# A two-layer transformer kernel: half of the first chunk's inverse loads issued from ScalarE's queue, and the next row's deviation taken between two steps of the last inversion

## The reference

```
h = layernorm(x) * (1 + ca) + sa
x = x + ga * attention_0(h)          # 16 heads of 8, causal softmax
h = layernorm(x) * (1 + cb) + sb
x = x + gb * experts_0(h)            # 8 experts, the top 2 of each token
h = layernorm(x) * (1 + ca) + sa     # second layer, own shifts and scales
x = x + ga * gated_delta_net(h)      # 12 heads, keys of 64, values of 128
h = layernorm(x) * (1 + cb) + sb
x = x + gb * ffn_1(h)                # 128 -> 512 -> 128, gelu
```

```
S = S * exp(gt); kv = kt . S; delta = (vt - kv) * bt
S = S + kt x delta; ot = qt . S
```

## Time and profile before

| | |
|---|---|
| median of three runs | 2789.67 us |
| the profiled execution | 2795.61 us |
| its span, first to last instruction | 2793.9 us |
| mean granted TensorE clock | 0.961 |
| TensorE busy (matmuls) | 2440.6 us, 87% |
| VectorE busy | 1793.1 us, 64% |
| ScalarE busy | 1453.6 us, 52% |
| GpSimd busy | 824.7 us, 30% |
| DMA engines, mean rate | 50 GB/s |

### The profile page before, as it was taken

The page is one execution under the profiler, slowest core; times in us unless marked ns, Lnnn a source line. Parts: engine busy times, 40 slices in busy tenths (PEclk is TensorE's granted clock), DMA queues, the critical chain, the costliest instruction groups (busy, mean ns, idle before and its releaser), DMA issues.

```text
span 2793.9 us, 65708 instructions
## 1 busy us (share of the span) xinstructions
PE 2440.6 (87%) x24090; PEld 1704.2 (61%) x24299; DVE 1793.1 (64%) x4697; ACT 1453.6 (52%) x3129; POOL 824.7 (30%) x581
## 2 busy tenths in 40 slices
PE   3898989899898988989889898898988989889997
PEld 2456755477554875547755577555774567655675
DVE  3467764777737766378664786557765678646776
ACT  0465534755448543385434754447544574446643
POOL 3045210552106511065100552015420253204521
PEclk8999999999999989999899998999999999999999
DMA  8201131010310103101130011300132011220113
GB/s 276 81 3 20 16 100 73 4 22 13 104 69 10 19 14 115 55 12 19 22 128 32 13 19 44 132 5 16 16 101 78 1 19 19 95 78 2 20 16 99
DMA packets 226986, 138.32 MB, mean 50 GB/s; under 512 B 173567, under 2 KB 209799, under 8 KB 219431
## 3 DMA queue, kind: packets, MB, share of 16 engines
q1 hardware_dynamic: 221670, 126.26, 16.1%
q10 hardware_dynamic: 4980, 7.60, 0.7%
HBM read 95.10 MB, written 38.71 MB: 48 GB/s over the span
## 4 chain that ended last, share of the span: by engine, by line
PE 50%; DVE 18%; ACT 15%; issue 9%; DMA 4%; SPq 3%; POOL 1%; DVEq 0%; ACTq 0%; POOLq 0%
PE bank L914 7%; PE bank L699 4%; PE bank L509 3%; PE bank L952 3%; PE bank L1013 3%; PE bank L690 3%; DVE small L1367 3%; PE bank L622 3%; ACT arena L1638 2%; ACT arena L1637 2%; PE bank L1033 2%; ACT vq L1645 2%; DVE blk_tx L1369 2%; DVE mx L1171 2%; PE bank L547 2%
## 5 line engine op out<-in xcount | busy, mean ns | idle before, releaser
L1912 POOL TENSOR_TENSOR arena<-upto,gk 128x1536 f32<-128x1536 f32 x32 | 88.1, 2752 | 679.2 <-DVE beta L1308 679.2
L1315 DVE SCALAR_TENSOR_TENSOR arena<-bank,conv,arena 128x510 f32<-128x510 f32 x320 | 237.1, 747 | 44.8 <-ACT arena L1638 27.2
L1171 DVE TENSOR_REDUCE mx<-bank 128x2 f32<-128x768 f32 (+3 forms) x187 | 202.1, 1123 | 56.6 <-PE bank L548 55.1
L509 PE MATMUL bank<-mask_k,ident_bf 128*128 128x512 bf16 x848 | 221.7, 389 | 17.4 <-issue 15.8
L1904 POOL TENSOR_TENSOR arena<-arena 128x511 f32<-128x511 f32 x160 | 201.6, 1270 | 56.8 <-DVE arena L1315 56.8
L1601 ACT ACTIVATE arena<-bank 128x384 f32<-128x384 f32 (+1 forms) x384 | 168.5, 547 | 49.1 <-PE bank L607 49.0
L760 PE MATMUL bank<-h_pad,arena 128*128 128x512 f32 x320 | 165.6, 615 | 28.5 <-DVE arena L1315 21.7
L547 PE MATMUL bank<-vq 128*128 128x128 bf16 (+3 forms) x528 | 122.0, 315 | 56.0 <-issue 35.7
L1367 DVE TENSOR_TENSOR small<-blk_tx,blk 96x1 f32<-96x1 f32 (+14 forms) x480 | 142.7, 297 | 16.5
L1622 ACT ACTIVATE arena<-bank,b1e 128x512 f32<-128x512 f32 x128 | 87.8, 686 | 116.8 <-PE bank L690 111.7
L1276 DVE SCALAR_TENSOR_TENSOR arena<-bank,comb,arena 128x128 f32<-128x128 f32 x256 | 72.1, 344 | 114.8 <-PE bank L699 113.7
(11 more groups left out here) (300 smaller groups left out, 5949.0 us busy)
## 6 DMA issues: line engine op xcount, KB each, us to landing
vq<-q_rows SPq DMA_DIRECT2D x18, 1024.0 KB, 8.5
vq<-k_rows SPq DMA_DIRECT2D x18, 1024.0 KB, 11.4
arena<-w_bounce SPq DMA_DIRECT2D x16, 1024.0 KB, 6.0
q_rows<-qkp SPq DMA_DIRECT2D x81, 128.0 KB, 2.4
k_rows<-qkp SPq DMA_DIRECT2D x81, 128.0 KB, 2.4
arena<-wv_rows SPq DMA_DIRECT2D x8, 768.0 KB, 10.2
ogt<-wv_rows SPq DMA_DIRECT2D x8, 768.0 KB, 11.8
t_bounce<-blk_tx SPq DMA_DIRECT2D x32, 192.0 KB, 2.1
```

The lines of the kernel that those rows point to most:

```text
L509: mm(PS[bank][:, :], ident_bf[:, :], mask_k[:, :, :].rearrange("p h w -> p (h w)"), start=True, stop=True)
L1171: V.reduce_max(dst, unit_scores(u), AX.X).then_inc(s_max, 1)
L1315: ins = V.scalar_tensor_tensor(a[:, k:T], ps[:, 0:T - k], conv[:, n, 3 - k:4 - k], a[:, k:T], ALU.mult, ALU.add)
```

## The change

There are two edits.

First, for chunk 0 alone, SP issues only the loads of the first four blocks. The other four are issued by ScalarE's queue, in a new function `load_inverses` that waits for `t_out` just as SP does. It is called right behind `direct(3)`. So that it can stand there, the copy that stood between `direct(3)` and the end of the loop moves behind it.

Second, ScalarE's `enter_stats` for the next row leaves its place behind `levels(3)` and is now called inside it, ahead of step 6.

```diff
@@ act_stages
-        act_stages += [("gate", 2), ("levels", 3), ("enter_stats", 1), ("rms", 2), ("enter_norm", 1), ("enter_h", 1), ("gate", 3),
+        act_stages += [("gate", 2), ("levels", 3), ("rms", 2), ("enter_norm", 1), ("enter_h", 1), ("gate", 3),
@@ ScalarE
+                def load_inverses():
+
+                    act.wait_ge(t_out, at(b, t_out, 16))
+                    for q in range(NBK // 2, NBK):
+                        r, d = slice(BS * q, BS * (q + 1)), slice(BS * q % DK, BS * q % DK + BS)
+                        act.dma_start(tx16[r, :, :, d].rearrange("p h s k -> p (h s) k"),
+                                      t_bounce[q].rearrange("h s i k -> i (h s) k")).then_inc(t_in, 16)
+
@@ convolve, ScalarE
-                        if n >= NQK + 2:
+                        if n >= NQK + 2 and n < NQK + 7:
                             copy_v(n - NQK - 2)
                         if n == NQK + 3:
                             first_tap(NCT - 1)
+                        elif n == NQK + 7:
+                            load_inverses()
                     if i == 2:
+                        copy_v(NTOK - 3)
                         copy_v(NTOK - 2)
                         copy_v(NTOK - 1)
@@ levels, ScalarE
                     for s in range(3, 8):
+                        if s == 6 and c + 1 == NT:
+                            enter_stats(b, 1)
@@ SP
-                    for q in range(NBK):
+                    for q in range(NBK if c else NBK // 2):
```

## The result

| | before | after |
|---|---|---|
| median, range, runs | 2788.68 us, 2783.77 to 2790.66, 4 | 2740.86 us, 2734.56 to 2749.12, 4 |
| the profiled execution, its span | 2795.61 us, 2793.9 us | 2734.56 us, 2732.8 us |
| mean granted TensorE clock | 0.961 | 0.976 |
| TensorE busy | 2440.6 us | 2433.6 us |

The ratio of after to before is 0.9834, 95% interval 0.9806 to 0.9862. The changed kernel is 47.8 us faster (38.5 to 54.1 by the interval). The forecast was 34.3 us; the time came out 4 us under the low end of the range.

The account below looks back on a forecast made before the run. TensorE was taken to bound the kernel, pausing for the first inversion's loads and the next row's normalised tokens. Gains of 17.1 + 17.2 = 34.3 us from the 2789.67 us median gave 2755 us, range 2745 to 2775.

Parts of the forecast that it names:

- both mechanisms: First inversion's loads: issues split over two queues, gain 17.1 us; next row's entry: earlier deviation, gain 17.2 us.
- the clock term: Behind both pauses: slow products may run faster once the pause is gone, 1.25 us a time; none counted.
- the bound of 27.2 us: Next row's entry: upper gain of the second edit if the pause makes the clock fall, 1.25 us more a time.
- the two terms: Clock terms at loads and entry; half of both, 5 + 5 us, gave the forecast's own low end, 2745 us.
- For the spread of the rows I leave 0.3 us a time: First inversion's loads: wait left after the first edit, cutting its gain from 19.5 to 17.1 us.
- the prediction's worst case of 3.8: First inversion's loads: a load lands at most 3.8 us after its issue began, leaving up to 0.75 us of wait.
- Rival A: First inversion's loads: the two queues take turns issuing, gain 3.6 us in place of 17.1, 2769 us; chance 0.20.
- Rival B: Next row's entry: the clock keeps half of the second gain, leaving 8.6 us, 2764 us; chance 0.13.
- Rival C: Behind either place: the gain comes back as another wait, at `blk` or the next chunk's mask, 2788 to 2790 us; chance 0.08.
- Rival D: First inversion's loads: long issues on ScalarE's queue hold its copies, kernel 7.8 us slower, 2797 us; chance 0.04.

## Why the prediction was right and where it was wrong

**The direction and both mechanisms were right.** Issuing was what was long at the loads, ScalarE's idle time hid its four issues, the deviation had its statistics before step 6, TensorE had nothing else to wait for, and no later wait took the gain back.

**The step that failed** is the clock term, at both places: "At most 8 x 1.25 = 10 us come back if the pause is gone. I count none of it." And for the second edit the bound of 27.2 us was written down and 17.2 taken. The prediction had read the clock at one place, behind the pause; ahead of it the clock was already at 0.51. The filled waits show that this term is real. At the loads it is 4.8 us, half of the 10, since in four of the eight rows the clock had not fallen. At the entry the pause itself is 17.2 us and the stages gave 31.1, so about 14 are clock, 12 of them behind the transposes; with the wait kept and filled 22 us came back behind the transposes, 16 net. The 14 are above the 10 us that the gate's products suggested: 8 us came back in the part with these products, 2 ahead of the transposes and 4 behind the next layer norm. The single timings of the second edit, 24 us, leave 7 for the clock. Sum of what was not counted: some 19 us by the stages. A row of full speed and a row of half speed for the same work stood beside each other in the evidence for the loads, and that was the ground to take half of the two terms at the least, which would have been 2745 us, the low end of the range.

**A second step was mis-sized the other way.** "For the spread of the rows I leave 0.3 us a time": it is 6.1 / 8 = 0.77 us. The issues began on time, but with two queues at work a load of ScalarE's lands a median of 2.6 us after its issue began, not 2.1, and its fourth, which ends the wait, 3.4 to 3.9 us after: near the prediction's worst case of 3.8 in every row, with a long issue or without. The pauses gave 13.4 us and not 17.1. The two errors partly cancel: 13.4 + 4.8 = 18.2 us at the first place, near the forecast's 17.1, for other reasons.

**Rival A,** two queues taking turns, is refuted: ScalarE's first three issues, 0.36 and 0.49 us long, lie in the same 1.4 us in which SP issued its own three. The trace does not show what the Trainium skill's "Perfetto Trace Analysis", section on the HWDGE DMA instruction, would lead to here, that a descriptor generator locked for one queue's instruction delays the other's. The rule of the Trainium skill's "DMA: Bandwidth & Descriptors", section "Issuing engines are not separate DMA queues", agrees with the trace: what was saved is issuing time, and a load did not land sooner (median 2.2 us for the first chunk's loads before, 2.1 for SP's and 2.6 for ScalarE's after). **Rival B,** half of the second gain lost to the clock, had the sign wrong in its sum: the work behind the transposes became 12 us shorter, not 8.6 us longer. What it feared did occur in part: the clock fell ahead of the pause in six of the 8 rows before, and a slow stretch is left at the entry in five of the 8 rows of the changed kernel. It is shorter: around the entry the clock was at half for 65 us over the rows before and for 24 after. **Rival C** did not occur: VectorE's second substitution starts 5.85 us behind the inversion's start (1226.27 - 1220.42), before 7.08 (1259.34 - 1252.26), so it came forward with the chain and more. **Rival D** did not occur with four loads and did with seven.

**Chance and place.** The inversion of the third chunk took 291.1 us in the profiled execution of before and 280.5 in that of after. Over kernels with that same place of the code it lies anywhere from 274.9 to 291.1 us, with either edit or none, so these 10.6 us lie within the scatter between executions and cannot be credited to the change. What they come from, a stall at that place of the program, is worth 15 us by the means of that stage.

**The best version** is the changed kernel with 8 unread products in the prologue, 2726.73 us, or with the rest of the pause filled, 2726.44; by their ratios of 0.977 and 0.978 they are one and the same. They are 14 to 16 us below the changed kernel's 2740.86 and 2742.84 as the times stand, and 14 to 24 by the ratios. Of that the stage of the third inversion gives 10 to 19 us, by the place of the code; no other stage got shorter.

**What stays open.** Which property of the place makes TensorE stall was not found; 8 and 16 instructions (a weight load and a product for each) work alike. The kernels before with 8 and 4 products gained 8 and 12 us in time where the stage gave 15, which is at or inside the ends of their intervals (2.5 to 15.3 and 8.1 to 21.5); nothing here tells whether a rest is missing. What makes the clock fall ahead of the entry's pause was not tried, nor where the long issue comes from, nor why ScalarE's fourth load lands late.

## What to carry to other kernels

Price a pause of TensorE as its length plus what the clock takes behind it: find the same products at full and at half speed in the trace, multiply the difference by how often the slow form occurs, and count that. Look also where the clock falls: at the entry it fell ahead of the pause in most rows, and part of the slow stretch stayed when the pause went. If a pause can't be shortened, filling it with unread products brings the second part alone (4.8 and 16 us here, beside 18 and 31 for removing it); size the fill by what it takes at half the clock, or it holds the work behind it, as it did here by 5 to 7 us. And before a gain of an added instruction is believed, put as many instructions where they do nothing: here a fill that seemed to bring 14 us brought none.

## What the runs showed of the hardware

SP's and ScalarE's queues issue DMAs at full pace at the same time (medians 467 and 490 ns); a long issue of 1.4 to 1.8 us then falls on the fourth of both at once in four of 8 rows, and ScalarE's fourth load lands 3.4 to 3.9 us after its issue began in all of them. In this kernel removing a pause of 2.2 us at the entry took off some 1.8 us more in slow products (14 us over 8 rows, from the stages of single executions). And 8 or 16 instructions more of TensorE in the prologue took 15 us off one stage of the loop (283.0 to 267.6, means of seven and six profiles), and 8 to 12 us off the median time of the kernel before; with them went a stall of 0.4 to 1.1 us between two products of the same step, and the low clock behind most of these stalls.
